# Packed transfers issued from GpSimd, and keys and values of later stages loaded in four parts

## The reference, cut to what matters

```python
qkv = (layernorm(x) @ qkv_w.T).reshape(B, T, 3, 16, 16)
q_dists = sum((q[..., None, :] - centers) ** 2, -1)        # k_dists in the same way
q_weights = exp(q_dists * inv_var)                         # k_weights in the same way
logits = einsum('bihs,bjhs,hs->bijh', q_weights, k_weights, amplitudes)
attention = softmax(logits / temp, axis=2)
x = x + einsum('bijh,bjhd->bihd', attention, v).reshape(B, T, D) @ out_w.T
...
xr, xk = mixtures of h = layernorm(x) and h one row earlier
x = x + sigmoid(xr @ W_r.T) * (square(relu(xk @ W_k.T)) @ W_v.T)
```

## Time and profile before

| | |
|---|---|
| median of 3 runs | 2278.15 us (2277.53 to 2280.14) |
| profiled execution, its own time | 2282.12 us |
| its span, first to last instruction | 2280.3 us |
| TensorE busy | 2169.9 us, 95% |
| ScalarE busy | 2005.4 us, 88% |
| VectorE busy | 906.9 us, 40% |
| GpSimd busy | 277.1 us, 12% |
| mean granted clock of TensorE | 0.990 of full speed |
| transfers | 180.27 MB, SP's queue at 31.2% of the 16 DMA engines |

### The profile page before, as it was taken

How to read it: one execution, slowest core, us unless ns; L and a number is a source line. 1 busy time by engine, 2 the same in 40 slices (tenths; PEclk the granted TensorE clock), 3 DMA queues, 4 the chain that set the end, 5 groups by cost and what they waited for, 6 DMA issues and landing times.

```text
span 2280.3 us, 46069 instructions
## 1 busy us (share of the span) xinstructions
PE 2169.9 (95%) x19886; PEld 897.8 (39%) x19886; DVE 906.9 (40%) x1777; ACT 2005.4 (88%) x2188; POOL 277.1 (12%) x260
## 2 busy tenths in 40 slices
PE   6699999999999999999999999999999999999997
PEld 4233433433443444444344444433433433333344
DVE  5233344334435352443525434352343243214435
ACT  3499999999989898999989999898999999998882
POOL 0121311311110111103011020110200000000000
PEclk9799999999999999999999999999999999999998
DMA  5723426226151431511533322430434130310110
GB/s 152 179 79 105 94 76 139 78 66 147 35 127 48 92 98 52 113 48 54 136 73 100 70 70 88 87 101 23 106 69 84 41 74 28 66 31 18 48 49 19
DMA packets 165582, 180.27 MB, mean 79 GB/s; under 512 B 82832, under 2 KB 108816, under 8 KB 162480
## 3 DMA queue, kind: packets, MB, share of 16 engines
q1 hardware_dynamic: 163264, 177.01, 31.2%
q10 hardware_dynamic: 2096, 0.14, 0.1%
HBM read 86.45 MB, written 75.89 MB: 71 GB/s over the span
## 4 chain that ended last, share of the span: by engine, by line
PE 76%; ACT 17%; DVE 3%; SPq 1%; DMA 1%; issue 1%; DVEq 0%
PE ps_pv L742 34%; PE ps_scores L725 22%; ACT probs L1050 16%; PE ps_step L770 16%; PE ps_step L787 2%; PE ps_scores L760 1%; PE ps_scores L755 1%; ACT weight L1114 1%; DMA gate_in<-x 1%; SPq L548 1%; DVE o_raw L1361 0%; DVE den_all L1476 0%; DMA q_parts<-parts 0%; PE ps_scores L765 0%; PE ps_scores L764 0%
## 5 line engine op out<-in xcount | busy, mean ns | idle before, releaser
L1050 ACT ACTIVATE probs<-ps_scores 128x1024 f32<-128x1024 f32 x2048 | 1934.7, 1035 | 184.6 <-PE ps_scores L725 180.4
L742 PE MATMUL ps_pv<-probs,vals 128*32 128x512 f32 x8192 | 1069.4, 606 | 12.3 <-DVE o_raw L1361 9.6
L725 PE MATMUL ps_scores<-q_aug,k_aug 49*128 49x512 f32 x4096 | 720.0, 441 | 41.7 <-ACT probs L1050 34.0
L725 PEld LDWEIGHTS ps_scores<-q_aug,k_aug 49*128 49x128 f32 x4096 | 336.5, 185 | 720.1 <-ACT probs L1050 683.7
L742 PEld LDWEIGHTS ps_pv<-probs,vals 128*32 128x32 f32 x8192 | 279.3, 141 | 289.1 <-issue 183.0
L1165 POOL TENSOR_TENSOR packed<-qk 32x512 f32<-32x512 f32 x224 | 243.3, 1086 | 905.9 <-DVE qk L1294 892.7
L1476 DVE RECIPROCAL den_all<-den_all 128x512 f32<-128x512 f32 x63 | 210.9, 3347 | 0.8
L1361 DVE COPY o_raw<-ps_pv 128x512 f32<-128x512 f32 x64 | 44.3, 692 | 318.4 <-PE ps_pv L742 318.4
L1170 POOL TENSOR_TENSOR k_act<-k_act 128x512 f32<-128x512 f32 x28 | 30.7, 1097 | 1004.9 <-DVE k_act L1297 1004.9
L1294 DVE COPY qk<-ps_step 128x512 f32<-128x512 f32 x56 | 38.7, 691 | 203.8 <-PE ps_step L770 203.8
L1269 DVE TENSOR_SCALAR weight<-ps_step,cen_sq 128x512 f32<-128x512 f32 x57 | 42.7, 749 | 160.7 <-PE ps_step L787 160.5
(11 more groups left out here) (202 smaller groups left out, 1014.4 us busy)
## 6 DMA issues: line engine op xcount, KB each, us to landing
q_aug<-q_parts SPq DMA_DIRECT2D x128, 192.0 KB
k_aug<-k_parts SPq DMA_DIRECT2D x30, 768.0 KB, 12.4
k_parts<-parts SPq DMA_DIRECT2D x32, 512.0 KB, 3.0
q_parts<-parts SPq DMA_DIRECT2D x32, 512.0 KB, 3.9
packed<-qk SPq DMA_DIRECT2D x224, 64.0 KB, 2.0
x_ffn<-x SPq DMA_DIRECT2D x18, 512.0 KB, 4.1
k_parts<-parts SPq DMA_DIRECT2D x32, 256.0 KB, 3.1
q_parts<-parts SPq DMA_DIRECT2D x32, 256.0 KB, 3.9
```

The costliest lines, as they stand in the source:

```text
L725: mm = pe.matmul(ps_scores[:, g % RING, e, :], k_aug[rows, s % 2, pair, kt * P:(kt + 1) * P], q_aug[rows, u % 2, pair, :], start=True, sto ...
L742: mm = pe.matmul(ps_pv[32 * c:32 * c + 32, :], vals[:, s % 2, kt, :, c], probs[:, tick % PROB_SLOTS, c, :], start=(kt == 0), stop=(kt == K ...
L1050: act.activation(probs[:, tick % PROB_SLOTS, 2 * pair:2 * pair + 2, :], ps_scores[:, g % RING, :, :], ACT.Exp).then_inc(probs_ready, 1)
```

## The change

POOL (GpSimd) issues the four packed transfers itself, after the wait for the copy and ahead of its four squares; SP no longer has them. Keys and values of all later stages are loaded in four parts of 512 keys, two ticks apart (one tick apart in the last stage, where there is less room), and the counts that the readers wait for are changed to match. The second stage's first part goes out at tick 20 instead of the whole at tick 1; the first parts of the others stay at the tick of the former whole load.

```diff
--- before.py
+++ after.py
@@ -245,7 +245,7 @@
 def stage_tick(b, s):
 
     before = (b, s - 2) if s >= 2 else (b - 1, s + 2)
-    tick = KT * (FINAL_UNIT[before] + 1) + 2 if before in FINAL_UNIT else 1
+    tick = KT * (FINAL_UNIT[before] + 1) + 2 if before in FINAL_UNIT else KT + 4
     if b or s >= 2:
         tick = max([tick] + [split_tick(*weighed(b, s, i), 1) + 4 for i in range(NC)])
     if b:
@@ -255,6 +255,12 @@
     tick = next((t for t in range(tick, last) if not any(t <= begin(task, "out0") - 5 < t + 9 for task in FFNS)), tick)
     assert tick < KT * FIRST_UNIT[b, s] - 10, (b, s, tick)
     return tick
+
+
+def part_tick(b, s, i):
+
+    first = stage_tick(b, s)
+    return first + min(2, (max_tick(b, s) - first) // (NC - 1)) * i
 
 
 def max_tick(b, s):
@@ -275,7 +281,7 @@
 
 LATER_STAGES = sorted([which for which in FIRST_UNIT if which != (0, 0)], key=FIRST_UNIT.get)
 STAGE_NO = {which: n for n, which in enumerate(sorted(FIRST_UNIT, key=FIRST_UNIT.get))}
-STAGE_AT = beside((stage_tick(b, s), (b, s)) for b, s in LATER_STAGES)
+STAGE_AT = beside((part_tick(b, s, i), (b, s, i)) for b, s in LATER_STAGES for i in range(NC))
 MAX_AT = beside((max_tick(b, s), (b, s)) for b, s in LATER_STAGES)
 QUERIES_AT = beside((queries_tick(u), u) for u in range(1, UNITS))
 LEAVE_AT = beside((KT * (u + 1) + 1, u) for u in range(UNITS - 1))
@@ -287,7 +293,6 @@
 
 X_AT = beside((max(begin(task, "turn0") - 18, 0), task) for task in NORMED)
 PREP_LN_AT = beside((max(begin(task, "turn0") - (8, 6, 5, 3)[part], 0), (task, part)) for task in NORMED for part in range(4))
-PACK_AT = beside((end(*which) + 1, which) for which in PROJECTED)
 WEIGH_AT = beside((weigh_gap(task, half, side), (task, half, side)) for task, half in WEIGHTS for side in range(2))
 SPLIT_AT = beside((split_tick(task, half, side), (task, half, side)) for task, half in WEIGHTS for side in range(2))
 PARTS_AT = beside((split_tick(task, half, 1) + 2, (task, half)) for task, half in WEIGHTS)
@@ -483,10 +488,6 @@
         def stage_count(b, s):
             return 2 * b + s // 2 + 1
 
-        def first_loads(s):
-
-            return NC - 1 if s % 2 == 0 else 0
-
         def copies_before(name):
 
             return sum(0 if of.startswith("dist") else 2 if of[0] in "kq" else 1 for of in FIRST[:FIRST_NO[name]])
@@ -563,7 +564,7 @@
                              ).then_inc(shifts_stored, 16)
 
             def max_pass(b, s, u):
-                sp.wait_ge(k_loaded[s % 2], LOADS_K * (stage_count(b, s) + first_loads(s)))
+                sp.wait_ge(k_loaded[s % 2], LOADS_K * NC * stage_count(b, s))
                 stage = STAGE_NO[b, s]
                 half, odd = s // 2, s % 2
                 again = LOADS_Q if stage else 0
@@ -643,17 +644,10 @@
                     store_attn(u)
                 for task, half in PARTS_AT.get(tick, ()):
                     store_parts(task[1], task[2], half, PARTS_BEFORE[task, half])
-                for task, name in PACK_AT.get(tick, ()):
-                    side = int(name[0] == "q")
-                    sp.wait_ge(step_free, STEP_NO[task, name] + 1)
-                    for c in range(4):
-                        b, a = divmod(c, 2)
-                        sp.dma_start(out=packed[64 * a:64 * a + 32, side, b, :], in_=qk[32 * c:32 * c + 32, side, :]
-                                     ).then_inc(packed_loaded[side], 16)
                 for task in V_AT.get(tick, ()):
                     sp.wait_ge(step_free, STEP_NO[task, "value1"] + 1)
                     store_v(*task[1:], v_rows, v_stored)
-                for b, s in STAGE_AT.get(tick, ()):
+                for b, s, i in STAGE_AT.get(tick, ()):
                     before = (b, s - 2) if s >= 2 else (b - 1, s + 2)
                     sp.wait_ge(parts_stored, stored_count(b, s, NC - 1) if b or s >= 2 else PARTS * FIRST_PARTS)
                     if b:
@@ -661,8 +655,8 @@
                     if before in FINAL_UNIT:
                         sp.wait_ge(scores_ready, 2 * KT * (FINAL_UNIT[before] + 1))
                         sp.wait_ge(pv_done, FINAL_UNIT[before] + 1)
-                    load_k(b, s, slice(0, T))
-                    load_v(b, s, 0, KT)
+                    load_k(b, s, slice(i * CHUNK, (i + 1) * CHUNK))
+                    load_v(b, s, TT * i, TT)
                 for b, s in MAX_AT.get(tick, ()):
                     with sp.If(unsafe == 1):
                         max_pass(b, s, FIRST_UNIT[b, s])
@@ -717,7 +711,7 @@
                 if g % (2 * KT) == 0:
                     pe.wait_ge(q_loaded[u % 2], LOADS_Q * (u // 2 + 1))
                     if u and u == FIRST_UNIT[b, s]:
-                        pe.wait_ge(k_loaded[s % 2], LOADS_K * (stage_count(b, s) + first_loads(s)))
+                        pe.wait_ge(k_loaded[s % 2], LOADS_K * NC * stage_count(b, s))
                 if u == 0 and pair == 0 and kt % TT == 0:
                     pe.wait_ge(k_loaded[0], LOADS_K * (kt // TT + 1))
                 for e in range(2):
@@ -734,7 +728,7 @@
                     if u:
                         pe.wait_ge(pv_free, u)
                     if u and u == FIRST_UNIT[b, s]:
-                        pe.wait_ge(v_loaded[s % 2], 16 * (stage_count(b, s) + first_loads(s)))
+                        pe.wait_ge(v_loaded[s % 2], 16 * NC * stage_count(b, s))
                 if u == 0 and kt % TT == 0:
                     pe.wait_ge(v_loaded[0], 16 * (kt // TT + 1))
                     pe.wait_ge(zeros_set, 3)
@@ -1159,6 +1153,10 @@
                     if (task, name) in SQUARE_NO:
                         side = int(name[0] == "q")
                         pool.wait_ge(step_free, STEP_NO[task, name] + 1)
+                        for c in range(4):
+                            b, a = divmod(c, 2)
+                            pool.dma_start(out=packed[64 * a:64 * a + 32, side, b, :], in_=qk[32 * c:32 * c + 32, side, :]
+                                           ).then_inc(packed_loaded[side], 16)
                         for c in range(4):
                             b, a = divmod(c, 2)
                             of = qk[32 * c:32 * c + 32, side, :]
```

## The result

The changed kernel took 2263.93 us in the median (2263.48 to 2264.74), against 2279.06 us for the kernel before in the same comparison: a ratio of 0.9935, 95% interval 0.9922 to 0.9947, a gain of 15.1 us (12 to 18). The forecast was 2270, within 2257 to 2284. The ratio is taken from runs of both kernels side by side; the other runs of the kernel before, behind the experiments, give medians of 2278.95 to 2280.66 us.

A forecast was written before the change was run, and what follows sets the result against it. TensorE, busy 95%, was taken as the bound, with one 17.7 us wait to win. 20.1 us gained less 12.0 paid, net 8.1, took the profiled 2282.1 to 2274.0, for the median 2270; range 2257 to 2284.

The forecast's parts named there:

- What bounds the kernel: TensorE, busy 95% of the span; the change can win only at its one 17.7 us wait, at distance step L787.
- t: Time of one packed-transfer issue on POOL, ahead of its squares: taken as 1.0 us, ends 0.5 and 2.0.
- full gain: Rival: POOL's issue as cheap as SP's (t up to 0.75), gain 14 to 20 us, 2258 to 2264; chance 0.24.
- the likeliest case: POOL's issue takes between 0.75 and 1.15 us, gain 4.6 to 14 us; chance 0.46.
- What stood beside t: A skill page's first byte of a GpSimd transfer, about 1 us against 0.6 from SP, set beside t = 1.0.
- The argument that SP's longest issue, 1.99 us, stood behind a full queue: Said against the slower case: POOL's own queue would not be full, so its issues would not take that long.
- The chain of sums behind t: Late chunks: POOL's start plus issues plus squares against due time; q waits 5.2, 2.5, 0.2 us at chunks 0, 1, 2.
- The clock term: Half clock on TensorE after new waits: 2.4 us lost at chunk 0 and 1.7 us at chunk 1.
- "Cost nothing" for the parts: Four-part loads on SP: 135 more issues, 56 us, against 132 us leaving SP; landing covered, so no cost.
- "The transfer lands 2.0 us after its issue, so it adds nothing": Packed transfers from POOL land before its squares are done, so landing adds no wait.
- The rule against the change: VectorE's two-port instructions lock out GpSimd's descriptor writing; chunk 1 would wait some 0.5 to 1 us longer, sum 7.5 us.
- The rivals of loss and of no difference: Slower: POOL's issue 1.4 us or more, chance 0.17. No difference: t near 1.25, 2274 to 2282, chance 0.13.

## Why the prediction was right, and where it was off

**What bounds the kernel** was read rightly. One wait of TensorE was all that could be won. 17.73 - 2.34 = 15.4 us of waiting went. The half clock went too: from one distance step to the next it is 99.43 - 2.34 - 94.29 = 2.80 us now, against 5.16, another 2.4 us. Together 17.8 of the 18.5 us between the two spans. Between the medians there are 15.1 us; the profiled execution of before was 3.1 us above its median, so a part of that gap is scatter. Such scatter goes with the mean granted clock: of 17 later runs of the kernel before on one chip, those at 0.989 and 0.990 took 2281.2 to 2284.9 us, those at 0.992 took 2274.1 to 2279.4.

**The cause** (the second stage's load ahead of the transfers) is shown by the run with the later tick alone: the load moved, the wait fell from 17.7 to 4.0 us.

**The step that was mis-sized is t**, "rounded to t = 1.0". The nearest row was taken to be POOL's instruction of 1.1 us on the same tile; it was SP's issue of the same transfer, 0.59 us, as the measured 0.50 us shows. The ends of 0.5 and 2.0 held, barely. At t = 0.5 the prediction's own sum gave some 18 us, and the "full gain" rival had 2258 to 2264, which the measured 2263.93 meets. So the number lies in the range because the range took in all values of t up to about 1.4: the likeliest case (chance 0.46) didn't come, its rival with 0.24 did. The run with doubled issues confirms the rest of the sum at the price that was assumed.

**What stood beside t.** The 1 us that the prediction set beside it is, in its own words, the time to the first byte of a transfer; t is the time that the issue holds the engine. These are two quantities, and that 0.6 us for the one and SP's 0.59 us for the other are alike shows nothing. The argument that SP's longest issue, 1.99 us, stood behind a full queue is not borne out: it lies at 440.2 us, and from 439.5 to 442.8 us the DMA engines were at a share of 0.21. The 56 us for SP's 135 further issues are 54 by the 0.4 us given, which changes nothing.

**The chain of sums behind t** was near: the wait at chunk 0's q by it is 1.2 us at t = 0.5, measured 2.34. 0.30 us between the end of k's squares and the first q issue, some 0.1 us between issues and squares twice, and 0.4 us less room at the first step (94.29 - 85.89 = 8.40 us, against 8.79) make 0.9 of the 1.1 us of difference. Chunks 1 and 2 don't wait, as they wouldn't at this t.

**The clock term** was too large for this profile. 1.7 to 2.4 us were set for each wait, but the wait of 2.34 us was followed by full clock. Nor was it too large everywhere: after the waits of 3.48 and 4.04 us in other runs the first work ran at 0.51 and 0.50. And full clock isn't safe: the second profile of the same kernel has the same wait and then 3.4 us at half clock (below).

**"Cost nothing" for the parts** was right for their cost and missed their use. Whole, the load at tick 20 makes chunk 1's transfers land after 9.3 to 10.5 us and TensorE wait 3.74 us. The prediction asked which work covers the load and not whom the load would hold up at its new place.

**"The transfer lands 2.0 us after its issue, so it adds nothing"** held at the waits of the full change (2.4 us in the median of all), and fails beside a large load. It also failed inside the full change, at no cost: at 1160.78 to 1169.2 us SP issued a later stage's four parts within 8.4 us, and the packed transfers from GpSimd beside them landed in 6.8 to 9.2 us, against 2.0 to 2.6 in the kernel before, where SP issued them ahead of the load. The order k, q, values, distances leaves room enough there, so TensorE didn't wait.

**The rule against the change** is that of the Trainium skill's page "SBUF — State Buffer", section "SBUF: two separate sides": VectorE in a two-port instruction locks GpSimd out of its descriptors. It has no visible effect: the four issues from 122.21 us on ran beside a cast of 0.36 us (123.21) and took 0.50 to 0.54 us each, landing in 1.9 to 2.0 us. The longest of all 224, 0.66 us, was the first, with VectorE idle. The cast is short, so this says nothing of longer instructions.

**The rivals of loss and of no difference** needed t from 1.25 up. The doubled issues, which are t = 1.0, still gained 7 us, so the order of the cases by t stands that far; above it nothing was run.

## What to carry to other kernels

When an engine with a full program waits long for a small transfer, look at what its queue issued just before, and whether that was wanted yet: a load of 2 MB wanted some 60 ticks later cost 17.7 us here, and moving it by one line gave most of the gain. Another queue was no way past a large load that was already on its way (8.7 to 13.0 us to land in place of 2); moving the load or splitting it was, as long as the parts go out apart: four of them within 8.4 us still held such transfers up to 9.2 us. Before pricing an issue from another engine, take the row of the same transfer on the engine that issues it now rather than the row of another operation on the new one, and when a load is moved, list the small transfers that it meets at its new place.

## What the runs showed of the hardware that was not expected

An issue from GpSimd took 0.50 us (496 ns at least, 662 at most, 224 of them), less than SP's 0.59 us in the median for the same transfer; the transfer landed in 2.4 us in the median, against 2.0 from SP. It occupies GpSimd for that time: doubling the issues moved its squares by 2.0 us a step.

Three transfers of 64 KB issued from GpSimd up to 1.1 us behind the start of a 2 MB load on SP's queue landed in 8.7, 11.7 and 13.0 us, one issued 0.4 us ahead of it in 1.9; four issued from 5.7 us behind such a load in 9.3 to 10.5 us; four behind a part of 512 KB in 4.0 to 5.3 us.

The clock after a short wait is not the same each time. Windows of the second profile of the full change, around the same wait of 2.33 us:

```profile
96.30:98.60 2.30, 0.00 (x0) 0.01 (x1) 0.00 (x0) 2.30 (x3) 2.07 (x2) 1.00 0.07 9
98.60:99.70 1.10, 1.08 (x20) 0.85 (x24) 0.00 (x0) 0.12 (x1) 0.00 (x0) 1.00 0.00 0
99.70:103.10 3.40, 3.40 (x18) 1.05 (x14) 0.75 (x1) 1.30 (x2) 0.00 (x0) 0.53 0.00 0
```

Here the granted clock is 0.53 for 3.4 us of work, 1.1 us after the wait; in the first profile it stayed at 1.00. By these windows that is 1.6 us (3.4 x 0.47) of difference between two executions of one kernel, from the clock alone.

The issue of the queries behind the 2 MB on SP's queue took 11.46 us in the kernel before and 12.06 with GpSimd's issue alone; behind a part of 512 KB it took 0.50, and with no load in front 0.31.
